# Causal attention with exps of 2048 columns out of one PSUM tensor of four banks, in place of 1024 columns out of two tensors of two

## The reference

```python
qkv = jnp.einsum('bsi,oi->bso', x, W_qkv)
Q, K, V = ...                     # split, to heads; rope on Q and K
scores = jnp.einsum('bhqd,bhkd->bhqk', Q, K) / jnp.sqrt(jnp.float32(d_k))
scores = jnp.where(causal, scores, -jnp.inf)
attn = jax.nn.softmax(scores, axis=-1)
out = jnp.einsum('bhqk,bhkd->bhqd', attn, V)
a = jnp.einsum('bsi,oi->bso', out, W_o)
x = _layernorm(x + a)
# then a linear layer with ternary weights on x quantized to 8 bits
x = _layernorm(x + jnp.einsum('bsi,oi->bso', x_dq, w) + bias)
```

## Time and profile before

| | us |
|---|---|
| median of 2 runs | 1852.61 (1848.75 to 1856.47) |
| profiled execution | 1846.45 |
| its span on the slowest core (core 3) | 1844.9 |
| spans of the eight cores | 1828.6 to 1844.9 |
| first exp of attention to last AV | 723 to 1543 |

### The profile page before, as it was taken

How to read it: one execution, slowest core, us unless ns; L and a number is a source line. 1 busy time by engine, 2 the same in 40 slices (tenths; PEclk the granted TensorE clock), 3 DMA queues, 4 the chain that set the end, 5 groups by cost and what they waited for, 6 DMA issues and landing times.

```text
span 1844.9 us, 18484 instructions; the slowest of 8 cores (1828.6 to 1844.9 us)
## 1 busy us (share of the span) xinstructions
PE 1182.9 (64%) x5064; PEld 386.5 (21%) x5064; DVE 630.8 (34%) x1208; ACT 974.6 (53%) x1195; POOL 30.6 (2%) x55
## 2 busy tenths in 40 slices
PE   0002776677777662677767787878788785656654
PEld 0001232232323230111111111112122221222221
DVE  0002233333333331554333322323212223566664
ACT  0002322221222442567888888888898896445443
POOL 0001000000000000000000000000000000000000
PEclk9999998888898996767999999999999998778777
DMA  9994633344333315222323313232311101022121
GB/s 104 123 161 100 112 77 78 92 94 89 95 83 86 83 46 122 59 78 87 102 76 109 109 55 109 73 125 74 141 72 72 72 1 46 23 69 69 46 69 46
DMA packets 112819, 153.31 MB, mean 83 GB/s; under 512 B 38736, under 2 KB 93008, under 8 KB 108368
## 3 DMA queue, kind: packets, MB, share of 16 engines
q1 hardware_dynamic: 65536, 113.26, 18.5%
q0 software_dynamic: 13648, 30.48, 11.5%
q10 hardware_dynamic: 33536, 8.39, 2.7%
HBM read 132.26 MB, written 46.14 MB: 97 GB/s over the span
## 4 chain that ended last, share of the span: by engine, by line
PE 36%; ACT 20%; DVE 16%; issue 11%; DMA 10%; another core or an unknown queue 3%; ACTq 3%; DVEq 1%; POOL 0%; SPq 0%; POOLq 0%
ACT exp_b L482 12%; PE pAV L504 10%; PE pSC L467 6%; DMA v_scr<-v_stg 6%; DVE exp_b L493 5%; PE pR L610 4%; PE pA L312 4%; PE pR L697 3%; ACT kraw L318 3%; PE pB L312 2%; DVE v_stg L390 2%; ACT recb L513 2%; PE pC L380 2%; DMA maskb<-masks 1%
## 5 line engine op out<-in xcount | busy, mean ns | idle before, releaser
L482 ACT ACTIVATE exp_b<-pSC 128x1024 bf16<-128x1024 f32 x640 | 606.0, 1053 | 144.5 <-PE pSC L472 121.2
L504 PE MATMUL pAV<-exp_b,v_run 128*128 128x512 bf16 x1280 | 415.5, 409 | 92.6 <-DVE exp_b L493 91.8
L493 DVE TENSOR_TENSOR exp_b<-exp_b,maskb 128x512 bf16<-128x512 bf16 x512 | 211.7, 425 | 364.5 <-ACT exp_b L482 306.4
L467 PE MATMUL pSC<-q_run,k_run 64*128 64x512 bf16 x640 | 253.3, 404 | 114.1 <-ACT exp_b L482 101.8
L472 PE MATMUL pSC<-q_run,k_run 64*128 64x512 bf16 x640 | 258.6, 413 | 0.0
L467 PEld LDWEIGHTS pSC<-q_run,k_run 64*128 64x128 bf16 x640 | 57.4, 94 | 412.0 <-issue 412.0
L318 ACT CAST kraw<-pA 128x512 bf16<-128x512 f32 x48 | 28.1, 586 | 210.6 <-PE pA L312 207.2
L504 PEld LDWEIGHTS pAV<-exp_b,v_run 128*128 128x128 bf16 x1280 | 77.2, 98 | 275.0 <-issue 275.0
L380 PE MATMUL pB<-w_kvT,x_T 128*128 128x512 bf16 x256 | 77.8, 472 | 35.8 <-DVE v_stg L390 35.8
L520 DVE TENSOR_TENSOR attn_n<-pAV,recb 64x512 bf16<-64x512 f32 x32 | 21.8, 683 | 213.2 <-ACT recb L516 211.9
L267 PE MATMUL pD<-identb,w_st 128*128 128x128 bf16 x32 | 4.1, 308 | 136.2 <-DVE w_st L261 136.2
(11 more groups left out here) (106 smaller groups left out, 1073.3 us busy)
## 6 DMA issues: line engine op xcount, KB each, us to landing
v_scr<-v_stg SPq DMA_DIRECT2D x32, 512.0 KB, 3.4
v_run<-v_scr SPq DMA_DIRECT2D x8, 2048.0 KB, 7.8
v_run<-v_scr SPq DMA_DIRECT2D x8, 1536.0 KB, 6.7
x_tm<-x_kv POOLq DMA_DIRECT2D x8, 1024.0 KB, 11.3
k_scr<-krot SPq DMA_DIRECT2D x64, 128.0 KB, 1.9
v_run<-v_scr SPq DMA_DIRECT2D x8, 1024.0 KB, 5.1
k_run<-k_scr SPq DMA_DIRECT2D x8, 1024.0 KB, 4.9
xo<-x_own SPq DMA_DIRECT2D x16, 512.0 KB, 4.4
```

Of the source, the lines that this page charges most:

```text
L467: s.add("T", (lambda sb_, bi, t: lambda te: te.matmul(pSC[sb_][:, 0:512], k_run[bi][0:64, t * 128:(t + 1) * 128], q_run[bi][0:64, :], star ...
L482: s.add("SC", (lambda eb, sb_: lambda sc: sc.activation(exp_b[eb][:, :], pSC[sb_][:, :], ACTF.Exp))(eb, sb_), reads=[f"pSC{sb_}"], writes= ...
L493: s.add("V", (lambda eb, moff, half: lambda v: v.tensor_tensor(exp_b[eb][:, half * 512:(half + 1) * 512], exp_b[eb][:, half * 512:(half + ...
L504: s.add("T", (lambda eb, bi, t, hh, n, pit: lambda te: te.matmul(pAV[pit][:, hh * 512:(hh + 1) * 512], v_run[bi][:, t * 256 + hh * 128: t ...
```

## The change

The key tiles are taken in blocks of two. `pSC` becomes a single tensor of 2048 columns in the same four banks, with two dependency keys, `pSCa` for the tile of even and `pSCb` for that of odd number. The exp of a block is one instruction over all 2048 columns, and it reads both keys. `exp_b` has two buffers of 2048 columns in place of three of 1024. Masks and AVs keep their shapes and work on halves of `exp_b`; the dependency key is that of the whole buffer. The order within an iteration becomes: scores of both tiles, exp of the block, masks of both tiles, AVs of the block before. The tail of the iteration before is added at block 2 (after its AVs), where it was at tile 4.

```diff
-            exp_b = [sbp(f"exp_b{i}", [128, 1024], BF16) for i in range(3)]
+            exp_b = [sbp(f"exp_b{i}", [128, 2048], BF16) for i in range(2)]
-            pSC = [psp(f"pSC{i}", [128, 1024], F32) for i in range(2)]
+            pSC = psp("pSC", [128, 2048], F32)
...
                 def emit_scores(t):
-                    sb_ = t % 2
-                    pk = f"pSC{sb_}"
+                    base = (t % 2) * 1024
+                    pk = "pSCa" if t % 2 == 0 else "pSCb"
...
-                def emit_exp(t):
-                    eb = t % 3
-                    sb_ = t % 2
-                    s.add("SC", (lambda eb, sb_: lambda sc: sc.activation(
-                        exp_b[eb][:, :], pSC[sb_][:, :], ACTF.Exp))(eb, sb_),
-                        reads=[f"pSC{sb_}"], writes=[f"exp_b{eb}"])
+                def emit_exp(bt):
+                    eb = bt % 2
+                    s.add("SC", (lambda eb: lambda sc: sc.activation(
+                        exp_b[eb][:, :], pSC[:, :], ACTF.Exp))(eb),
+                        reads=["pSCa", "pSCb"], writes=[f"exp_b{eb}"])
 
                 def emit_mask(t):
                     if t < n - 8:
                         return
-                    eb = t % 3
+                    eb = (t // 2) % 2
+                    base = (t % 2) * 1024
...
                 def emit_av(t):
-                    eb = t % 3
+                    eb = (t // 2) % 2
+                    base = (t % 2) * 1024
                     ek = f"exp_b{eb}"
...
-                for t in range(n):
-                    emit_scores(t)
-                    emit_exp(t)
-                    emit_mask(t)
-                    if t >= 2:
-                        emit_av(t - 2)
-                    if t == 4 and pending_tail is not None:
+                for bt in range(n // 2):
+                    t0, t1 = 2 * bt, 2 * bt + 1
+                    emit_scores(t0)
+                    emit_scores(t1)
+                    emit_exp(bt)
+                    emit_mask(t0)
+                    emit_mask(t1)
+                    if bt >= 1:
+                        emit_av(t0 - 2)
+                        emit_av(t1 - 2)
+                    if bt == 2 and pending_tail is not None:
                         emit_tail(*pending_tail)
                         pending_tail = None
                 emit_av(n - 2)
```

More of the change, by code:

```diff
@@ L464, in emit_scores @@
                 def emit_scores(t):
-                    sb_ = t % 2
-                    pk = f"pSC{sb_}"
-                    s.add("T", (lambda sb_, bi, t: lambda te: te.matmul(
-                        pSC[sb_][:, 0:512], k_run[bi][0:64, t * 128:(t + 1) * 128],
+                    base = (t % 2) * 1024
+                    pk = "pSCa" if t % 2 == 0 else "pSCb"
+                    s.add("T", (lambda base, bi, t: lambda te: te.matmul(
+                        pSC[:, base:base + 512], k_run[bi][0:64, t * 128:(t + 1) * 128],
                         q_run[bi][0:64, :], start=True, stop=True,
-                        tile_position=(0, 0), skip_group_check=True))(sb_, bi, t),
+                        tile_position=(0, 0), skip_group_check=True))(base, bi, t),
                         reads=[kk, qk], writes=[pk])
-                    s.add("T", (lambda sb_, bi, t: lambda te: te.matmul(
-                        pSC[sb_][:, 512:1024],
+                    s.add("T", (lambda base, bi, t: lambda te: te.matmul(
+                        pSC[:, base + 512:base + 1024],
                         k_run[bi][64:128, t * 128:(t + 1) * 128],
                         q_run[bi][64:128, :], start=True, stop=True,
-                        tile_position=(64, 0), skip_group_check=True))(sb_, bi, t),
+                        tile_position=(64, 0), skip_group_check=True))(base, bi, t),
                         reads=[kk, qk], writes=[pk])
-                def emit_exp(t):
-                    eb = t % 3
-                    sb_ = t % 2
-                    s.add("SC", (lambda eb, sb_: lambda sc: sc.activation(
-                        exp_b[eb][:, :], pSC[sb_][:, :], ACTF.Exp))(eb, sb_),
-                        reads=[f"pSC{sb_}"], writes=[f"exp_b{eb}"])
+                def emit_exp(bt):
[3 more added lines that the diff above has]
+                        reads=["pSCa", "pSCb"], writes=[f"exp_b{eb}"])
                 def emit_mask(t):
@@ L492, in emit_mask @@
                     for half in range(2):
[L493 to L496, removed]
+                        s.add("V", (lambda eb, base, moff, half: lambda v: v.tensor_tensor(
+                            exp_b[eb][:, base + half * 512:base + (half + 1) * 512],
+                            exp_b[eb][:, base + half * 512:base + (half + 1) * 512],
+                            maskb[:, moff:moff + 512], ALU.mult))(eb, base, moff, half),
                             reads=[f"exp_b{eb}", "maskb"], writes=[f"exp_b{eb}"])
                 def emit_av(t):
-                    eb = t % 3
+                    eb = (t // 2) % 2
+                    base = (t % 2) * 1024
                     ek = f"exp_b{eb}"
@@ L503, in emit_av @@
                     for hh in range(2):
-                        s.add("T", (lambda eb, bi, t, hh, n, pit: lambda te: te.matmul(
+                        s.add("T", (lambda eb, base, bi, t, hh, n, pit: lambda te: te.matmul(
                             pAV[pit][:, hh * 512:(hh + 1) * 512],
                             v_run[bi][:, t * 256 + hh * 128: t * 256 + (hh + 1) * 128],
-                            exp_b[eb][:, hh * 512:(hh + 1) * 512],
+                            exp_b[eb][:, base + hh * 512:base + (hh + 1) * 512],
                             start=(t == 0), stop=(t == n - 1),
-                            skip_group_check=True))(eb, bi, t, hh, n, pit),
+                            skip_group_check=True))(eb, base, bi, t, hh, n, pit),
                             reads=[ek, vk], writes=[f"pAV{pit}"])
```

## The result

| | before | after |
|---|---|---|
| median, us | 1848.74 (10 runs, 1845.82 to 1871.11) | 2167.92 (11 runs, 2161.21 to 2186.69) |
| ratio | | 1.173, 95% interval 1.170 to 1.176 |
| profiled execution, us; its slowest core | 1846.45; core 3, span 1844.9 | 2166.92; core 4, span 2165.4 |

A forecast was written before the change was run, and what follows sets the result against it. ScalarE's exps were taken to bound unmasked attention; joining the buffers makes scores and exp alternate. Serial loops, masked stalls, tails and iteration ends add 247 us (full clock) to 408 (half), mixed 327: span 2172, time 2173 us, range 2080 to 2270.

The forecast's parts named there:

- The forecast case: Attention with TensorE's clock mixed between full and half: 327 us more, 2173 us in all, own range 2120 to 2225; chance 0.62.
- exp of 2048 columns: ScalarE's exp of one block, extrapolated from 512 and 1024 columns: 1.885 us, with 1.83 and 2.05 as ends.
- loop at full clock: One block, scores and exp strictly alternating: exp 1.885, to scores 0.15, scores 0.60, to exp 0.18, together 2.815 us.
- loop at half clock: The same serial block with TensorE at half clock, scores taking 1.03 us: 3.245 us.
- iteration's end: Next iteration's scores queue behind the last block's masks and AVs: ScalarE idles 4.06 us at full clock, 5.29 at half.
- granted clock, attention: TensorE's mean clock level over attention, taken as 0.75, a little above the 0.71 of slot 0 before.
- iteration, slots 0 to 3: Attention's four slots, eight iterations each of 4, 8, 12, 16 blocks: 15.99 to 49.77 us full clock, 18.45 to 57.39 half.
- AV lies under the exp: Four AVs of the block before take 1.02 us (full) or 1.82 (half), covered by the exp of 1.885.
- The stall in the masked run: Masked blocks' AVs wait for all four masks, delaying scores two blocks on: 0.315 us full, 0.685 half, once an iteration.
- Full clock (2093): Rival: the loop keeps TensorE working, so attention stays at full clock, 247 us more; 2093 us, chance 0.14.
- half clock (2254) throughout: Rival: gaps in every block hold TensorE at half clock, 408 us more; 2254 us, chance 0.20.
- the loop isn't serial: Rival: next scores start before the wide exp ends, or double buffering is worth nothing; about 1855 us, chance 0.04.

## Why the prediction was right, point by point

The forecast case came, at 2168 us against 2173. Term by term:

| term, us | predicted | measured |
|---|---|---|
| exp of 2048 columns | 1.885 | 1.877 |
| loop at full clock | 2.815 | 2.74 |
| loop at half clock (gap 1.34 or 1.28, and 1.88) | 3.245 | 3.22 or 3.16 |
| iteration's end, half clock | 5.29 | 5.27 |
| iteration's end, full clock (with added matmuls) | 4.06 | 4.01 |
| granted clock, attention | 0.75 | 0.80 (0.64, 0.75, 0.83, 0.86 by slot) |
| iteration, slots 0 to 3 (mean of both clocks) | 17.2, 29.3, 41.5, 53.6 | 18.2, 29.8, 41.0, 51.8 |

- *The exp.* Extrapolating from 512 and 1024 columns was good to 0.01 us. Neither bound, 1.83 or 2.05, was needed.
- *The loop.* Right in its parts but for one. From the scores' end to the exp I took 0.18 us, from a single pair of scores. Behind the second pair it is 0.10 in the loop, with the scores' end as modelled.
- *AV lies under the exp.* Held at both clocks: in unmasked runs the scores start 0.14 us after the exp's end at either clock (at half clock exp's end 1666.59, scores 1666.73), so AVs held nothing back.
- *Masks and iteration ends.* Right where the clock is one level throughout. What I missed is that these are the very places at which TensorE waits long and the clock is down. The stall in the masked run was to be 0.32 at full clock and 0.69 at half. It was 2.06 - 1.34 = 0.72 in slot 0 (second view below), but 2.53 - 0.92 = 1.61 in the row of slot 3 above: there the loop had run at full clock, and AVs and scores behind the mask wait ran at half.
- *The clock.* One share for all slots was the wrong shape. In slot 3 the loop of 2.74 us held full clock for eight blocks on end with TensorE idle for 1.16 us in each (first view below). In slot 0 the mean was 0.64. So the long slots came out shorter and the short slots longer than forecast. The forecast was too low by 1.0 and 0.5 us in slots 0 and 1 and too high by 0.4 and 1.8 in slots 2 and 3, and eight of each cancel to 6 us. The terms cancel in the same way. The 230 gaps of plain loops had a mean of 0.99 us, so such a loop took 2.87, where the forecast's mean of both levels is 3.03: too much, by some 45 us over 288 loops. The iteration's end took 5.2 us or more in 27 of 31 cases, half clock, where the forecast's mean is 4.68: too little, by 17 us over 31 ends. The masked stalls added some 34 us to their gaps where 16 were forecast. That the total is right to 0.3% is luck in this part; the mechanism and the terms at either level don't hang on it.

```profile
1625.00:1648.00 23.00, 12.55 (x65) 3.61 (x64) 1.31 (x4) 15.88 (x9) 0.00 (x0) 1.00 0.00 0
```

```profile
783.75 1.88 ACT L481 ACTIVATE exp_b<-pSC 128x2048 bf16<-128x2048 f32 x1 [2.06 <-PE pSC L472]
```

- *Idle time before exps.* "Some 350 us in all" was a slip and not from the sum. What the profile shows is 31 iteration ends (162 us), 230 gaps in plain loops (227), 25 gaps with a masked stall (58), 2 at the tails, and 15.9 us for the first load of the masks, which the kernel before had too (17.3): 465.
- *The rivals.* Full clock (2093) and half clock (2254) throughout didn't come. That the loop isn't serial is refuted by every block: scores start 0.14 us after the exp's end, or later. The Trainium skill (TensorE: Matmul & The Clock Gate, "HAM oscillation — how this bites in real kernels") says of one kernel that PSUM double buffering gave nothing more. That does not carry over: here one narrow buffer in place of two costs 479 us (2327.7 - 1848.9), since ScalarE had no idle time in the unmasked runs to begin with. The Trainium skill (same page, "A second HAM failure mode: psum-queue depth-cycling") says of another kernel that short idles between groups of matmuls made the clock swing. Slot 0 agrees, with 0.64; the eight blocks of slot 3 at full clock, each with TensorE idle for 1.16 us, show that short idles need not do it.

## What to carry to other kernels

Widening an instruction by joining the two halves of a double buffer buys the fixed part of an instruction (5 us of ScalarE time in all here) and pays with the overlap (190 to 250 us). Before doing it, count the closed loop of hand-overs that is left, and see whether the engine that is widened has idle time at all. Where both buffers are kept, look at the queue order behind them: letting the consumer of the last tile stand three tiles later, across the end of an iteration, took 107 us off a kernel that was bound by ScalarE in its unmasked runs.

## What the runs showed of the hardware

A wait can cost twice: once by itself, and once by TensorE's level behind it. Shortening waits by about 40 us (by the count at full to half clock) brought 84, with the granted clock up by about 0.1; and 832 matmuls that do nothing made the kernel 41 us faster, with the clock of slot 0 at 0.96 in place of 0.65. An exp of 2048 columns out of four PSUM banks took 1.877 us, against 0.917 us from start to start for exps of 1024 back to back. So the wide form saves next to nothing on ScalarE: its 320 exps are busy for 600.7 us and the 640 narrow ones for 606.0.
